# Two gate sets per matmul group in a pair of LSTM recurrences, with another spread of the input projections and a smaller lag between the layers

## The reference

```python
x_proj = jnp.einsum('ntd,df->ntf', x, Wx) + b          # (2, 2048, 2048)
def step(carry, xp_t):
    prev_h, prev_c = carry
    h_bar = xp_t + prev_h @ Wh                          # (2, 512) @ (512, 2048)
    i = jax.nn.sigmoid(h_bar[:, 0:Hdim])
    f = jax.nn.sigmoid(h_bar[:, Hdim:2 * Hdim])
    o = jax.nn.sigmoid(h_bar[:, 2 * Hdim:3 * Hdim])
    g = jnp.tanh(h_bar[:, 3 * Hdim:4 * Hdim])
    next_c = f * prev_c + i * g
    next_h = o * jnp.tanh(next_c)
    return ((next_h, next_c), next_h)
...
x = x + _L2_cond_ref(x, cond_1024, L2_cond_Wx, L2_cond_Wh, L2_cond_b)
x = x + _L3_cond_ref(x, cond_1024, L3_cond_Wx, L3_cond_Wh, L3_cond_b)
```

## Time and profile before

| | us |
|---|---|
| median of 3 runs (lowest, highest) | 11977.81 (11977.42, 11978.15) |
| profiled execution | 11977.42 |
| its span in the trace | 11975.6 |
| PE busy | 11867.9 (99%) |
| PEld busy | 2759.4 (23%) |
| DVE busy | 8157.7 (68%) |
| ACT busy | 3094.3 (26%) |
| POOL busy | 1423.1 (12%) |

### The profile page before, as it was taken

One profiled execution on the slowest core, in us unless ns is written; L12 is line 12 of the kernel. 1 busy time (PEld: TensorE's weight loads), 2 busy tenths in 40 slices (PEclk: granted clock), 3 DMA queues, 4 the chain that ended last, 5 costly groups with the idle time before them and its releaser, 6 DMA issues.

```text
span 11975.6 us, 416297 instructions
## 1 busy us (share of the span) xinstructions
PE 11867.9 (99%) x231988; PEld 2759.4 (23%) x100916; DVE 8157.7 (68%) x34052; ACT 3094.3 (26%) x20602; POOL 1423.1 (12%) x5238
## 2 busy tenths in 40 slices
PE   8999999999999999999999999999999999999998
PEld 5222222222222222222222222222222222222222
DVE  2567777767776777677677776767677667776765
ACT  2222222222222222222222222222222222222221
POOL 4011111111111111111111111111111111111110
PEclk9999999999999999999999999999999999999999
DMA  4000000000000000000000000000000000000000
GB/s 163 24 4 5 4 4 5 4 4 5 4 4 4 5 4 5 5 4 5 5 4 5 5 4 5 5 4 4 5 4 4 5 4 4 5 4 4 5 4 3
DMA packets 374389, 106.60 MB, mean 9 GB/s; under 512 B 349594, under 2 KB 357830, under 8 KB 372436
## 3 DMA queue, kind: packets, MB, share of 16 engines
q1 hardware_dynamic: 362372, 61.96, 2.8%
q0 software_dynamic: 3504, 11.56, 0.3%
q10 hardware_dynamic: 6560, 6.32, 0.2%
HBM read 62.98 MB, written 16.78 MB: 7 GB/s over the span
## 4 chain that ended last, share of the span: by engine, by line
PE 96%; DVE 2%; issue 1%; ACT 1%; DVEq 0%; POOLq 0%; POOL 0%
PE bank L80 87%; PE bank L872 7%; PE bank L518 1%; PE bank L531 1%; DVE gates_t L1050 1%; DVE pre L1055 0%; ACT tanh_c L948 0%; ACT sig L943 0%; DVE prod L1062 0%; DVE state L1073 0%; DVE state L1069 0%; DVE gc L1065 0%; DVE state L1076 0%; ACT gc L944 0%; PE bank L484 0%
## 5 line engine op out<-in xcount | busy, mean ns | idle before, releaser
L80 PE MATMUL bank<-wh,state 128*6 128x512 bf16 x196608 | 11321.2, 379 | 61.7 <-DVE state L1076 60.5
L1050 DVE STREAM_TRANSPOSE gates_t<-bank 128x512 f32<-128x512 f32 x4096 | 2936.8, 717 | 678.4 <-PE bank L80 194.6
L80 PEld LDWEIGHTS bank<-wh,state 128*6 128x6 bf16 x65536 | 1560.4, 85 | 6426.9 <-issue 5968.9
L943 ACT ACTIVATE sig<-pre 128x16 f32<-128x16 f32 x4096 | 885.0, 216 | 6944.4 <-DVE pre L1055 6944.4
L1062 DVE TENSOR_TENSOR prod<-sig,gc 128x16 f32<-128x16 f32 x4096 | 717.8, 175 | 1217.8 <-ACT gc L944 1065.8
L1069 DVE TENSOR_TENSOR state<-sig,tanh_c 128x8 f32<-128x8 f32 x4096 | 689.8, 168 | 1124.5 <-ACT tanh_c L948 1124.5
L948 ACT ACTIVATE tanh_c<-gc 128x8 f32<-128x8 f32 x4096 | 854.5, 209 | 1711.5 <-DVE gc L1065 1711.4
L1055 DVE TENSOR_REDUCE pre<-gates_t 128x24 f32<-128x96 f32 x4096 | 1036.6, 253 | 139.4
L979 POOL TENSOR_TENSOR x<-x1r,state 128x8 f32<-128x8 f32 x2048 | 435.6, 213 | 5435.1 <-DVE state L1076 5435.1
L979 POOL TENSOR_TENSOR y<-x,state 128x8 f32<-128x8 f32 x2048 | 434.7, 212 | 4974.0 <-DVE state L1076 4974.0
L872 PE MATMUL bank<-wx,x 128*32 128x128 f32 x16384 | 799.8, 273 | 0.0
(11 more groups left out here) (119 smaller groups left out, 1685.7 us busy)
## 6 DMA issues: line engine op xcount, KB each, us to landing
w<-in_w SPq DMA_DIRECT2D x8, 2048.0 KB, 13.1
out<-y_rows SPq DMA_DIRECT2D x1020, 8.0 KB, 1.8
wx<-in_x SPq DMA_DIRECT2D x16, 512.0 KB, 5.3
x1p<-x_t_all SPq DMA_DIRECT2D x128, 64.0 KB, 2.6
x1r<-x_t_all SPq DMA_DIRECT2D x128, 64.0 KB, 2.6
x_t_all<-wx ACTq DMA_DIRECT2D x6, 1024.0 KB, 4.8
wx<-in_Wh POOLq DMA_DIRECT2D x8, 512.0 KB, 4.2
wx<-in_Wh POOLq DMA_DIRECT2D x16, 256.0 KB, 4.5
```

Source lines behind the costliest of these rows:

```text
L80: return pe.add_instruction(mybir.InstMatmult(name=nc.get_next_instruction_name(), engine=mybir.EngineType.PE, ins=[pe.lower_ap(moving), p ...
L943: act.activation(sig[l][:, 0:2 * HB], pre[l][:, 0:2 * HB], ACT.Sigmoid)
L1050: dve.transpose(gates_t[l][:, :, NS * NB:], gates[l][:, 0:NMS * C].rearrange("p (m c) -> p m c", c=C)).then_inc(s["trans"], 1)
```

## The change

Two numbers and one table change; the code that reads them does not.

```diff
-NS = 1
+NS = 2
 NMS = NM // NS
 SPAN = PARTS * NS * NB
...
-SUMS = ((0,) * 8 + (2,) * 8, (2,) * 8 + (0,) * 8)
-
-LAG = CH + 8 + 1
+SUMS = ((0, 0, 2, 2) + (1,) * 12, (8, 8) + (0,) * 14)
+
+LAG = CH + 2 + 1
 
 ROWS_AT = LAG - CH + 1
```

## The result

| | before | changed |
|---|---|---|
| median of the runs, us | 11977.98 (4 runs) | 12060.24 (4 runs) |
| lowest, highest | 11977.42, 11981.31 | 12059.23, 12063.70 |
| span of the profiled execution | 11975.6 | 12057.5 |

The ratio is 1.0067, with a 95% interval of 1.0055 to 1.0080: the changed kernel is slower by 0.67%, 82 us. The forecast was 12046 (+0.57%), with a range of 11995 to 12110. The same kernel run again beside later experiments gave 12059.67 and 1.0069 (1.0055 to 1.0082).

What follows compares the result with a forecast made beforehand. TensorE's paired steps (5.62 us) were taken to bound the kernel, by a hair over one layer's loop (5.61). +122 - 2 - 36 - 4 - 12 - 0.2 = +68 gave 12046 us, range 11995 to 12110.

Steps and rivals of the forecast that it cites:

- Term 1: TensorE's recurrent product: 24 rounds of 256 columns for 12 of 512, 2.62 us a step for 2.59: +122 us.
- first rival: TensorE's product: a round halves fully to 107.9 ns, the step stays 2.59 us: 11924 us; chance 7%.
- fourth rival: TensorE's product: instruction starts or weight loads bind, 3.2 us a step: 14400 us; chance 3%.
- Term 2: One layer's loop: the product's transpose on DVE shrinks to 0.44 us, reductions unchanged, loop 5.61 to 5.37 us.
- Term 3: Projection units respread over paired steps: a one-unit pair takes 5.46 us on TensorE, above the loop; unit-free pairs -2 us.
- second rival: Paired steps: the transpose doesn't shrink, so the 5.64 us loop binds one-unit pairs: 12320 us; chance 4%.
- third rival: Projection burst: TensorE waits in step 1 of each chunk for the first quarter's transpose: 12135 us; chance 5%.
- Term 4: Lag 25 to 19: six more paired steps, 12 fewer single ones, -36 us; remaining single steps -4 us.
- Term 5: Scattered delays in paired steps, 33 us: a third should go through the loop's slack, -12 us.
- Term 6: Weights cut on POOL into two sets, 24 more instructions: no effect on the time.
- tail: The kernel's end: -0.2 us.

Runs made afterwards that it cites:

- half rounds: The kernel before, with each 512-column matmul cut into two of 256; transpose, reductions, units and lag unchanged: 12098.60 us, ratio 1.0101.

## Why the prediction was right

**Term 1, twice the rounds (+122): right.** Measured by itself it is +121.5. The left-over of 2.5 ns for each round of four matmuls, read from two stretches of the front, carried over to a stretch of other data and other shapes. That rules out the first rival, which needed a round of 107.9 ns; the step's 2.62 us are 109.2 a round. The loads cost nothing that can be measured. The fourth rival, a step of 3.2 us for its 128 starts, is refuted: they take 2.62 us, 20.5 ns each on average, and the four matmuls of a round start only 3 to 4 ns apart. The prediction took this rival from the 25 ns between starts in the Trainium skill ("TensorE: Matmul & The Clock Gate", section "Wait — 56ns, not 53.3ns?"); with four column tiles the trace does not agree with it.

**Term 2, the loop (5.61 to 5.37): right in its mechanism, wrong in its size.** The transpose fell to 450 ns (0.44 forecast), but the loop only to 5.45. The step that failed is "The reductions have the same 96 and 32 elements, state and gates the same sizes: unchanged." They took 72 and 22 ns more, and the first of these stands in the loop. A count of elements says nothing of how they lie: the four terms of a sum now stand 16 bytes apart, where before two of them lay within 16 bytes. The Trainium skill ("SBUF — State Buffer", section "Specifications (TRN2)") says that SBUF has lines of 16 bytes, that each step to a new line costs, and that two hits in a line are needed for full speed. The trace agrees: 8 bytes apart 253 ns, 4 bytes apart 253, 16 bytes apart 325. This rule was at hand, and the code says how far apart the terms stand.

**Term 3, the units' places: right.** A pair with one unit takes 5.46 us and is TensorE's. It holds by 5.46 - 5.45 = 0.01 instead of 0.09: by these numbers, had the first reduction cost 20 ns more, TensorE would have waited in 12 of 16 pairs. The spread alone, with the old loop, shows what that costs: 5.61 for 5.40, the second rival's mechanism. The burst of eight units stalls nothing in paired steps; the third rival took place in two single steps, at 0.4 us each, one of them at 388.40, where DVE does not have a whole product's time ahead.

**Term 4, the lag and the singles (-36 and -4): right.** Both single stretches gave -70.0, for -67.3 - 4 forecast; 24 singles at 5.45 instead of 5.37 come to 1.9 us, which covers the 1.3 between them.

**Term 5, stalls (-12): right for the delays it speaks of (-12), partly by luck.** By the starts of TensorE's rounds the scattered delays in paired steps add up to 33 us before (114 of them) and to 21.5 after (86). The slack of the pairs with one unit, which was to take most of them, is 0.01 where 0.09 was forecast (term 2), and 81 of the 86 stand in such pairs. Pairs with two or sixteen units, a quarter of all, have 0.23 us and more, and only 5 delays come through there. Had the reductions kept their length, the delays would have fallen further, to 14.5, as the experiment with neighbouring terms shows. The timeline of the changed kernel at one delay, DVE first, then PE:

```profile
1885.84 0.17 DVE L1062 TENSOR_TENSOR prod<-sig,gc 128x16 f32<-128x16 f32 x1 [0.69 <-ACT gc L944]
```

```profile
1881.31 5.42 PE L80 MATMUL bank<-wh,state 128*12 128x256 bf16 x192
...
1887.12 3.12 PE L80 MATMUL bank<-wh,state 128*12 128x256 bf16 x108 [0.17 <-DVE state L1076]
```

`prod` began at 1885.84, after 0.69 us of idle time; in the turn before (at 1882.63) it was 0.34. TensorE then starts the pair after 5.81 us for 5.46: the whole delay of 0.35 arrives.

**Term 6 (nothing) and the tail: as forecast.** The step that failed beside term 2: what the sum has at nothing without a reason is the end of each round of the hardware loop. The prediction priced twice the instructions by the share of queue q8 alone (0.7 to 1.3%, which came true). At a jump they cost more: TensorE waits 2.34 us, and a product at a granted clock of 0.59 follows. All such places together cost 11.3 us for 2.5, +8.8.

The forecast's sum was 14 us low. Of these 9 are the places of the hardware loop and some 3 the longer reductions (1.3 in the single stretches, 1.4 in the 18 pairs without units). The remaining 2 are not accounted for. All of this is small beside the +122 of term 1, so the forecast could hold in spite of two steps that failed.

## What to carry to other kernels

Cutting a group of matmuls into twice as many of half the columns is paid for by a fixed left-over per round (2.5 ns here), and what one gets back on the consumer's side (a transpose shorter by 0.27 us) counts only where the consumer's loop is what ends last; here TensorE and the loop were level, and TensorE was the one made longer. A kernel with twice the instructions for the same work can also pay where its hardware loop jumps back: here some 4 us each time on TensorE, so a loop with long rounds should be the cheaper one, which no run here tried. Shortening the loop of one layer without touching TensorE's work was the better half of the idea: splitting the transpose gave 0.13% where the change lost 0.67%. And when a layout changes, look up the distance between the elements that an instruction reads one after another, not only their number.

## What the runs showed of the hardware that was not expected

- A reduction of 96 fp32 in SBUF takes 253 ns with the added terms 4 or 8 bytes apart and 325 ns with 16; of 32 elements, 176 and 198 ns.
- DVE's instructions are late at some places, in all versions, mostly by 0.18 or 0.36 us. Of before's 70 such delays in mid-turn all lie at three places in blocks of 128 of DVE's records, one for each round of the hardware loop, and they stay there when 40 instructions are put ahead. The pages of before and of the split transpose, a queue that fetches instructions:

```profile
q14 instruction: 640, 5.24, 0.1%
```

```profile
q14 instruction: 672, 5.51, 0.2%
```

  A packet is 8.2 KB (5.24 MB by 640). The split transpose adds 4096 instructions to DVE, and the queue 32 packets: 128 instructions each. So the period of the delays is that of this queue's packets. TensorE's queue, q8, has packets of 16.4 KB (21.51 MB by 1313 in the earlier trace rows); the changed kernel adds 262,144 matmuls and loads, and the queue 1023 packets: 256 instructions each. The Trainium skill ("Runtime: NRT & Kernel Launch", section "Instruction fetch mechanics") says that instructions are refilled in blocks of 16 KiB, 256 instructions, and that crossing a block is mostly hidden. TensorE's packets agree with the 256. On DVE the period is 128, and the delays show, some 33 us of the kernel before, where the loop of one layer and TensorE are level.
- Where the hardware loop jumps, TensorE waits 1.9 to 2.9 us at the first jump ("issue") in every kernel here with 96 matmuls in a step, and in none with 48, where DVE is the late one. In the changed kernel a 16 KB packet of q8 starts at 4288.52, during the product ahead of the wait, and takes 1.2 us. That TensorE waits for its instructions is likely, but no run shows it.
- After 2.34 us of idle time at the jump the granted clock of the next product is 0.59 of full on average, so most of it ran at the lower level (1.2 GHz), and it takes 4.28 us for 2.62. After the 1.93 us of the half rounds the product takes 2.62.
- With four column tiles a step's 96 matmuls and 32 loads start 20.5 ns apart on average, the four of a round 3 to 4 ns, and doubling the loads at the same matmuls changes the time by 1.8 us in 12100.
